# Stacked rounded latents and a one-pass key projection in an attention and expert kernel

## The reference, cut to what matters

```python
q = (x @ Wq + bq).reshape(B, T, H, D)
kv_latent = gelu(x @ Wkd + bkd)            # 64 columns
lat = kv_latent[..., :32] + kv_latent[..., 32:]
kv = lat @ Wku + bku                       # 32 rows, 256 columns
k, v = kv[..., :C], kv[..., C:]
attn = softmax(causal(q k^T * scale)); out = attn @ v
```

## Time and profile before

| | us |
|---|---|
| median of 3 runs | 648.69 |
| the runs | 646.8, 648.73, 648.69 |
| the profiled execution | 646.88 |
| its span in the trace | 645.0 |
| TensorE busy | 599.1 |
| VectorE busy | 542.1 |
| ScalarE busy | 487.6 |
| GpSimd busy | 167.7 |

### The profile page before, as it was taken

One profiled execution on the slowest core, in us unless ns is written; L12 is line 12 of the kernel. 1 busy time (PEld: TensorE's weight loads), 2 busy tenths in 40 slices (PEclk: granted clock), 3 DMA queues, 4 the chain that ended last, 5 costly groups with the idle time before them and its releaser, 6 DMA issues.

```text
span 645.0 us, 10999 instructions
## 1 busy us (share of the span) xinstructions
PE 599.1 (93%) x3297; PEld 441.4 (68%) x3297; DVE 542.1 (84%) x1338; ACT 487.6 (76%) x858; POOL 167.7 (26%) x144
## 2 busy tenths in 40 slices
PE   8799889888999999999999999785898999999996
PEld 5466556555545688888888888354675888888884
DVE  4868888888858868988988888869799789999997
ACT  5658999999647899999999999798635556666663
POOL 4422323223304033553455342040432000000000
PEclk9899999999998999999999999996897999999998
DMA  7000000000100042112201210000000222222201
GB/s 252 1 1 3 1 3 1 1 0 1 34 1 0 6 164 99 52 47 99 98 29 68 98 49 1 1 1 1 0 1 2 69 91 89 91 90 90 91 0 67
DMA packets 6491, 28.83 MB, mean 45 GB/s; under 512 B 862, under 2 KB 990, under 8 KB 4383
## 3 DMA queue, kind: packets, MB, share of 16 engines
q1 hardware_dynamic: 6448, 28.32, 12.4%
HBM read 27.13 MB, written 1.19 MB: 44 GB/s over the span
## 4 chain that ended last, share of the span: by engine, by line
PE 63%; DVE 24%; ACT 6%; issue 4%; DMA 1%; POOL 0%; SPq 0%; DVEq 0%; ACTq 0%; POOLq 0%
PE PS L1213 17%; PE PS L1215 16%; PE PS L1214 16%; DVE STAT L874 9%; PE PS L1364 2%; PE PS L1292 2%; DVE RA L894 2%; PE PS L1319 2%; PE PS L1239 2%; DVE SU L900 1%; DVE HN L680 1%; PE PS L1333 1%; ACT STAT L397 1%; DVE HL L692 1%; ACT RA L635 1%
## 5 line engine op out<-in xcount | busy, mean ns | idle before, releaser
L1015 DVE TENSOR_TENSOR RA<-AR,RA 128x512 fp32r<-128x512 f32 x144 | 137.4, 978 | 26.2 <-ACT RA L518 24.6
L517 ACT ACTIVATE AR<-PS,BI 128x512 f32<-128x512 f32 x144 | 99.8, 693 | 15.3 <-PE PS L1215 7.8
L1213 PE MATMUL PS<-HH,WH 128*128 128x512 f32 x272 | 108.9, 400 | 0.2
L1215 PE MATMUL PS<-HL,WH 128*128 128x512 f32 x272 | 107.1, 394 | 0.0
L1214 PE MATMUL PS<-HH,WL 128*128 128x512 f32 x272 | 107.1, 394 | 0.0
L518 ACT ACTIVATE RA<-PS,BI 128x512 fp32r<-128x512 f32 x144 | 98.7, 685 | 0.0
L874 DVE CUSTOM_DVE_ANT_0 STAT<-PS,MQ 128x128 f32<-128x128 f32 (+1 forms) x256 | 76.3, 355 | 20.0 <-PE PS L1320 19.9
L1213 PE MATMUL PS<-RA,WH 128*128 128x512 f32 x208 | 83.0, 399 | 3.7 <-DVE RA L1179 2.1
L1215 PE MATMUL PS<-RA,WH 128*128 128x512 f32 x208 | 81.2, 391 | 0.0
L1214 PE MATMUL PS<-RA,WL 128*128 128x512 f32 x208 | 81.2, 391 | 0.0
L320 POOL TENSOR_TENSOR AR<-AR 128x512 f32<-128x512 f32 x32 | 50.8, 1587 | 113.2 <-DVE AR L827 113.2
(11 more groups left out here) (212 smaller groups left out, 1164.3 us busy)
## 6 DMA issues: line engine op xcount, KB each, us to landing
AR<-comb SPq DMA_DIRECT2D x15, 1024.0 KB, 4.7
WS<-in_w SPq DMA_DIRECT2D x9, 512.0 KB, 5.5
WS<-in_w SPq DMA_DIRECT2D x7, 384.0 KB, 3.1
M<-in_mats SPq DMA_DIRECT2D x1, 1384.0 KB, 10.8
X<-in_xT SPq DMA_DIRECT2D x4, 256.0 KB, 4.4
out_xT<-X SPq DMA_DIRECT2D x4, 256.0 KB, 2.1
AR<-in_wmod SPq DMA_DIRECT2D x1, 768.0 KB, 7.8
AR<-in_w SPq DMA_DIRECT2D x1, 384.0 KB, 3.1
```

Of the source, the lines that this page charges most:

```text
L517: act.activation(G[:, c, :], PS[:, c, :], ACT.Gelu_apprx_tanh, bias=bias).then_inc(s["act"], 1)
L1015: dve.tensor_tensor(out=GL[:, m0 % 2, c, :], in0=G[:, c, :], in1=f(GH[:, m0 % 2, c, :]), op=ALU.subtract).then_inc(s["lo"], 1)
L1213: pe.matmul(out, wh, xh, start=first, stop=False)
L1215: return pe.matmul(out, wh, xl, start=False, stop=last)
```

## The change

The latents are no longer kept as the gelu's two halves in plain f32. The gelu goes to `LG`. A selection matmul (`three_rows`, `pick` in columns 640 to 737 of `KM`) writes the sum of the halves three times, and two rows of ones, to 98 rows of PSUM. One instruction (VectorE for block 0, ScalarE for blocks 1 to 3) rounds it into `LATR`, and one of VectorE makes `LAT` in fp32r: rounded, rest, rounded. The key and value weights get the matching rows (`KMS`: rounded, rounded, rest) by two VectorE instructions. One fp32r matmul of 98 rows then gives the split product. The latents of blocks 1 to 3 are made after the first projection. `LL` is made in four quarters in the steps 28 to 31 of the last expert instead of at the start.

```diff
-        KM = sb("KM", [65, 640])
+        LG = AR[0:65, 8192:10240]
+        KM = AR[0:98, 2048:2786]
+        LAT = RA[0:98, 3072:5120]
+        KMS = RA[0:98, 5120:5760]
+        KMR = RA[0:98, 5760:6400]
+        LATR = RA[0:98, 6400:7936].rearrange("p (r n) -> p r n", r=3)
+        SUM_BANK, VALUE_BANK = (0, 4, 2, 3), (5, 4, 2, 3)
 # GpSimd
+            gp.wait_ge(l_done, 1)
             gp.tensor_scalar(LH[:, :], lm, 1.0, 0.0, ALU.mult, ALU.add).then_inc(l1_split, 1)
-            gp.wait_ge(l1_split, 1)
-            gp.wait_ge(hn_done, 8)
-            gp.tensor_tensor(out=LL[:, :], in0=lm, in1=f(LH[:, :]), op=ALU.subtract).then_inc(l1_split, 1)
 # GpSimd, experts, after acc(m, ...)
+                    if m >= 28 and ne == 9:
+                        gp.wait_ge(l1_split, 1)
+                        part = slice((m - 28) * MATS["l1"] // 4, (m - 27) * MATS["l1"] // 4)
+                        gp.tensor_tensor(out=LL[:, part], in0=lm[:, part], in1=f(LH[:, part]), op=ALU.subtract)\
+                          .then_inc(l1_split, 1)
 # ScalarE
+            def rounded_latents(t):
+                act.wait_ge(sel_psum, t + 1)
+                if t == 3:
+                    act.wait_ge(l_done, 1)
+                act.activation(LATR[:, t % 3, :], PS[0:98, SUM_BANK[t], :], ACT.Copy, scale=vec("lat_sign")[0:98, :])\
+                   .then_inc(lr_more, 1)
             evac_proj(0, 0)
+            for t in range(1, NBLK):
+                rounded_latents(t)
             evac_proj(1, 1)
 # VectorE, before the modulation is copied
+            dve.tensor_scalar(KEPT[:, :], bias, vec("q_keep"), None, ALU.mult).then_inc(qk_bias, 1)
+            dve.tensor_scalar(SIGNED[:, :], bias, vec("q_sign"), -1.0, ALU.mult, ALU.mult).then_inc(qk_bias, 1)
+            dve.wait_ge(flipped, 2)
+            dve.tensor_scalar(KMR[:, 0:640], KM[:, 0:640], vec("w_sign")[0:98, :], None, ALU.mult).then_inc(kms_done, 1)
+            dve.wait_ge(kms_done, 1)
+            dve.scalar_tensor_tensor(out=KMS[:, 0:640], in0=KM[:, 0:640], scalar=vec("w_keep")[0:98, :], in1=f(KMR[:, 0:640]),
+                                     op0=ALU.mult, op1=ALU.subtract).then_inc(kms_done, 1)
 # VectorE, the latents
+            def latents(t):
+                if t == 0:
+                    dve.wait_ge(sel_psum, 1)
+                    dve.tensor_scalar(LATR[:, 0, :], PS[0:98, 0, :], vec("lat_sign")[0:98, :], None, ALU.mult)\
+                       .then_inc(lr_done, 1)
+                    dve.wait_ge(lr_done, 1)
+                else:
+                    dve.wait_ge(lr_more, t)
+                dve.scalar_tensor_tensor(out=blk(LAT, t), in0=PS[0:98, SUM_BANK[t], :], scalar=vec("lat_keep")[0:98, :],
+                                         in1=f(LATR[:, t % 3, :]), op0=ALU.mult, op1=ALU.subtract).then_inc(l_done, 1)
-            all_values(0)
-            all_values(1)
+            latents(1)
+            latents(2)
             maxima(0, 0, 0)
-            all_values(2)
+            latents(3)
             maxima(0, 0, 1)
             spread_max(0, 0)
+            all_values(0)
             with_max(0, 0)
-            all_values(3)
+            for j in range(1, 4):
+                all_values(j)
 # TensorE
+            def three_rows(t):
+                if t == 0:
+                    pe.wait_ge(in_k, 16)
+                    pe.wait_ge(latent_one, 1)
+                pe.wait_ge(lat_done, t + 1)
+                pe.matmul(PS[0:98, SUM_BANK[t], :], KM[0:65, 640:738], blk(LG, t), start=True, stop=True).then_inc(sel_psum, 1)
+            latent(0)
+            latent(1)
+            three_rows(0)
+            latent(2)
+            latent(3)
 # in project
-                pe.matmul(PS[:, 6, 256:512], KM[:, 128 * g:128 * g + 128], LAT[:, cols], start=True, stop=True)\
+                pe.matmul(PS[:, 6, 256:512], KMS[:, 128 * g:128 * g + 128], LAT[:, cols], start=True, stop=True)\
 # order before the first step
             project(0, 0, 0)
-            (16 value matmuls)
+            for t in range(1, NBLK):
+                three_rows(t)
             scores(0, 0, 0)
             project(1, 1, 0)
             scores(0, 0, 1)
             project(2, 2, 0)
-            keep_clock(8)
+            (16 value matmuls, fp32r, each four after l_done)
+            keep_clock(4)
             maxima_t(0, 0)
 # layer 1
-            pe.wait_ge(l1_split, 2)
+            pe.wait_ge(l1_split, 5)
```

More of the change, by code:

```diff
@@ L15 @@
 VECS = dict(bo=1, bq=4, q_sign=1, q_keep=1, k_keep=1, b1=4 * E0, b2=E0, pb=4, gb=3, fb=3,
-            outb=1, alpha=1, norm=1, norm2=1, bkd=1, c=16, prio=8)
+            outb=1, alpha=1, norm=1, norm2=1, bkd=1, c=16, prio=8,
+            w_sign=1, w_keep=1, lat_sign=1, lat_keep=1)
 MATS = dict(wkd=64, wq=512, wo=512, router=8, wg=8, l1=4 * 128 + 3 * 384)
@@ L92, in build @@
         ON = AR[:, 0:8192].rearrange("p (g n) -> p g n", g=4)
-        LAT = AR[0:65, 8192:10240]
+        LG = AR[0:65, 8192:10240]
+        KM = AR[0:98, 2048:2786]
         VALL = AR[:, 10240:12288].rearrange("p (i c) -> p i c", i=16)
@@ L155, in build @@
         latent_one = sem("latent_one")
+        kms_done, sel_psum, lr_done, lr_more, l_done = map(
+            sem, ("kms_done", "sel_psum", "lr_done", "lr_more", "l_done"))
         p1_psum, p1_done, a_done, asq_done, sa_done, hsi_done, sqrt_done, s_ready, scan_done, hs2_mul, hs2_done = map(
@@ L420, in _ @@
                 act.wait_ge(kd_done, t + 1)
-                act.activation(LAT[0:64, t * BLK:(t + 1) * BLK], PS[0:64, t, :], ACT.Gelu, bias=vec("bkd")[0:64, :])\
+                act.activation(LG[0:64, t * BLK:(t + 1) * BLK], PS[0:64, t, :], ACT.Gelu, bias=vec("bkd")[0:64, :])\
                    .then_inc(lat_done, 1)
@@ L829, in moe_scale @@
                    .then_inc(s["ymul"], 1)
-            dve.memset(LAT[64:65, :], 1.0).then_inc(latent_one, 1)
+            dve.memset(LG[64:65, :], 1.0).then_inc(latent_one, 1)
             dve.wait_ge(in_vec, 16)
@@ L834, in _ @@
                 centre(0, t)
+            bias = V[:, VAT["bq"]:VAT["bq"] + 4]
+            dve.tensor_scalar(KEPT[:, :], bias, vec("q_keep"), None, ALU.mult).then_inc(qk_bias, 1)
[5 more added lines that the diff above has]
+                                     op0=ALU.mult, op1=ALU.subtract).then_inc(kms_done, 1)
             dve.wait_ge(mod_psum, 1)
@@ L856, in _ @@
                 normalise(0, t)
+            def latents(t):
[8 more added lines that the diff above has]
+                                         in1=f(LATR[:, t % 3, :]), op0=ALU.mult, op1=ALU.subtract).then_inc(l_done, 1)
+            latents(0)
             def all_values(j):
@@ L1282, in _, with latent @@
             pe.wait_ge(in_mats, 16)
-            for t in range(NBLK):
+            def latent(t):
                 pe.wait_ge(hn_done, 2 * t + 2)
@@ L1391, in step @@
                     values(n - 1, n0 - 1, it)
-            pe.wait_ge(in_k, 16)
-            pe.wait_ge(lat_done, 1)
-            pe.wait_ge(latent_one, 1)
             pe.wait_ge(flipped, 4)
+            pe.wait_ge(kms_done, 2)
+            pe.wait_ge(l_done, 1)
             project(0, 0, 0)
[L1398 to L1403, removed]
+            for t in range(1, NBLK):
+                three_rows(t)
             pe.wait_ge(ident_done, 9)
@@ L1410, in _ @@
             project(2, 2, 0)
-            keep_clock(8)
+            for i in range(16):
+                if i % 4 == 0:
+                    pe.wait_ge(l_done, i // 4 + 1)
+                mm = pe.matmul(PS[:, VALUE_BANK[i // 4], 128 * (i % 4):128 * (i % 4) + 128],
+                               LAT[:, 128 * i:128 * i + 128], KMS[:, 512:640], start=True, stop=True)
+                if i % 4 == 3:
+                    mm.then_inc(v_psum, 1)
+            keep_clock(4)
             maxima_t(0, 0)
@@ L1681, in layouts @@
     put("bkd", a["L0_attn_bkd"])
+    put("w_sign", np.repeat(np.array([-1, -1, 1, -1, 1], f4), [32, 32, 32, 1, 1]))
+    put("w_keep", np.repeat(np.array([0, 0, 1, 0, 1], f4), [32, 32, 32, 1, 1]))
+    put("lat_sign", np.repeat(np.array([-1, 1, -1, -1], f4), [32, 32, 32, 2]))
+    put("lat_keep", np.repeat(np.array([0, 1, 0, 0], f4), [32, 32, 32, 2]))
     put("c", np.concatenate([a["L0_c"], a["L1_c"]]).T)
@@ L1694, in layouts @@
     wk = np.concatenate([heads(a["L0_attn_Wku"][:, :128], 3).reshape(32, 512), a["L0_attn_Wku"][:, 128:]], 1)
+    bias = np.concatenate([bk.reshape(1, 512), np.zeros((1, 128), f4)], 1)
+    pick = np.zeros((98, 98), f4)
+    pick[np.arange(192) % 64, np.arange(192) // 64 * 32 + np.arange(192) % 32] = 1.0
+    pick[64, 96:98] = 1.0
     rows = np.concatenate([a["L0_attn_bku"][128:], a["L0_ffn_router_b"]])
@@ L1704, in layouts @@
         mats=mats,
-        kmats=np.concatenate([wk, wk, np.concatenate([bk.reshape(1, 512), np.zeros((1, 128), f4)], 1)]),
+        kmats=np.concatenate([np.concatenate([wk, wk, wk, bias, bias]), pick], 1),
         rows=np.tile(rows, (128, 1)),
```

5 lines of the change are left out of this document (1 added, 4 removed).

## The result

The changed kernel takes 654.65 us (median of 4 runs, 654.22 to 658.81), beside 648.71 for the kernel before (646.8 to 649.72, 4 runs). The ratio is 1.0122, 95% interval 1.0098 to 1.0146: slower by 1.2%. Forecast were 650.3, a range from 646.0 to 652.8, and 0.39 for slower. The medians lie 5.9 us apart, where 1.6 were forecast. The direction of the forecast was right; the time lies outside the range.

What follows compares the result with a forecast made beforehand. Steady attention steps were taken as bound by VectorE, the start as serial, the experts' end as VectorE's. 646.88 + 1.1 - 0.3 + 1.6 = 649.3, plus half of the 1.9 between two run levels: 650.3 us, range 646.0 to 652.8.

Steps and rivals of the forecast that it cites:

- 1. One-pass key projection: Attention steps: 0.32 us less TensorE work per unit, worth nothing in steady steps, -0.3 over steps 0 to 2.
- 2. The start: Weights, latents and values before the first attention step: +1.1 us in sum, from +0.5 to +2.0.
- (b): When line 894 first runs: TensorE's clock falls near 30.5 and returns near 35, landing it between 36.1 and 36.9.
- -0.15: First run of line 894, against 36.65 before: forecast shift in us, from -0.55 to +0.25.
- 1.2 + 2.8 + 1.1: Before the first transposes: us for projection 2, sixteen value matmuls and four clock-keeping ones, mostly at 1.2 GHz, from 31.4.
- the order of `all_values`: Between line 894 and the first step: two more `all_values` of 0.65 each, +1.3 us.
- the two about the clock: Rivals at the start: clock stays up, 648.7 us, chance 0.22; clock late before the matmul at 20.7, 653, chance 0.08.
- The weights at 13.8: VectorE makes KMR and KMS before copying the modulation, moving that copy by about +0.6 us, 0 to +1.0.
- 3. `LL` in quarters: End of layer 0's experts: quarters 0 and 1 free, 2 costs +0.6, 3 costs +1.0; sum +1.6 us, +0.3 to +2.1.
- forecast +0.8: Up to the last attention unit: the start's +1.1 us and the key projection's -0.3 taken together.

Runs made afterwards that it cites:

- e11_before_dense: Kernel before, with two clock-keeping matmuls added ahead of scores(0,0,1) and three ahead of project(2): 646.79 us, ratio 0.9974.
- e6_v32: Changed kernel with its 16 value matmuls read as plain f32, two records each, instead of one-pass fp32r: 655.42 us, ratio 1.0126.
- e8_keep8: Changed kernel with eight clock-keeping matmuls behind the values instead of four: 656.76 us, ratio 1.0143.
- e2_values: Changed kernel with all four `all_values` ahead of `with_max` of unit 0, instead of one ahead and three behind: 654.27 us, ratio 1.0132.
- e7_all: Changed kernel with eight clock-keeping matmuls before the first scores, all `all_values` ahead of `with_max`, and `LL` quarters in steps 26 to 29: 649.65 us, ratio 1.0024.
- e13_dense_k32: e9_dense with the key projection read as plain f32 in all 32 units: 646.28 us, ratio 0.9981.
- e4_before_ll: Kernel before, with only `LL` made in four quarters in steps 28 to 31 instead of one instruction at 22 us: 648.73 us, ratio 1.0031.
- e1_fill: Changed kernel with eight clock-keeping matmuls where TensorE idles before the first scores: 652.68 us, ratio 1.0094.
- e5_fill_k32: e1_fill with the key projection read as plain f32 in every unit: 653.6 us, ratio 1.0075.
- e9_dense: e7_all with two more clock-keeping matmuls ahead of scores(0,0,1) and two ahead of project(2): 644.36 us, ratio 0.9952.

## Why the prediction was wrong, point by point

**1. One-pass key projection: mechanism right, size smaller.** Steady steps were worth nothing, as forecast: 125.34 against 125.36 for 27 units, and the two passes put back changed neither. The -0.3 for the steps 0 to 2 was too much: with the clock up, two passes and one give 18.05 and 18.07.

**2. The start. The step that failed is (b)**, "I expect the clock to fall at about 30.5 and to come back at about 35". It fell at 28.7 behind the idle time foreseen (the values' 3.73 us gone from 24.32), but it did not come back until 56. That the fall needs this gap is not shown: in e11_before_dense the clock fell at 28.6 with the values in place and 0.52 us idle. I had also read the fall in the kernel before as following three mostly idle microseconds; its trace shows TensorE busy for 1.00, 0.64 and 0.20 of the last three. My 35 was copied from the kernel before, without its matmuls: there TensorE came back to two f32 projection halves and eight long matmuls; here it came back to one f32 and one one-pass half, 16 short one-pass matmuls and four long ones. With the old values (e6_v32) or the old eight (e8_keep8) the clock returned by the first step; without the idle 1.58 us it did not (e2_values, e7_all). What decides on it stays open. I priced the lower clock for the matmuls ahead of line 894 alone, and took the steps behind it at 2.4 GHz. Line 894 came at 38.62, not at 36.1 to 36.9 (+1.97 on 36.65 in place of -0.15): my 1.2 + 2.8 + 1.1 from 31.4 ends ahead of the transposes, and measured were 1.24, 3.30, 1.82 and another 0.66 for the transposes, from 31.60. From there to unit 4 it took 24.96 instead of 18.75: +6.2. Of these 4.8 are the clock: e6_v32 and e8_keep8, which have the changed order and the clock back by the first step, take 20.20. The remaining 1.45 are the order of `all_values` (forecast +1.3). No rival held this: the two about the clock had it stay up, or come back late by one stretch at 20 us. What would have shown it: at half clock a step takes 6.66 (units 1 to 2, against 4.40), so that an uncertain return was worth 2.3 per step and not 1 us in all.

The weights at 13.8 cost 0.04 instead of 0.6 in this execution, since KMR and KMS took 0.55 and 0.88 and their data came no later than before. Elsewhere they did cost: in e13_dense_k32 TensorE had finished the modulation at 13.96, and the copy, behind KMS, started at 14.81.

**3. `LL` in quarters: right.** Forecast +1.6, measured +1.17 from step 30 to `centre`, in the changed kernel and alone (e4_before_ll); from unit 31 on it is +1.54 and +1.16, where the scatter ahead of step 30 comes in. A quarter takes 1.26 to 1.53, not 1.0, which my one row of 1664 columns undersized. Where it costs was right: 0.35 in step 30, 0.82 in the residual adds. Moved two steps ahead, the quarters cost 0.96 less up to `centre`; whether they cost anything there can't be told, since the kernels without them scatter by more.

**The sum.** 646.88 + 1.1 - 0.3 + 1.6 = 649.3 against 654.22 for the profiled execution. By terms: +8.16 up to the last unit (forecast +0.8), +1.54 to `centre` (forecast +1.6, and 1.17 of it the quarters'), and -2.3 in layer 1, where the recurrence's wait fell otherwise on the clock, which no term of mine held.

## What to carry to other kernels

Work taken off TensorE is not only worth its time: what it did for the clock goes with it. Here two ways of putting some of it back saved 4.8 us in the steps, at a cost of 2.4 ahead of them. Before such an edit, list TensorE's idle gaps in the new order, and price a fall of the clock for as long as the stage behind it lasts, not up to the next matmul. Filling one gap of several leaves it to chance (e1_fill, e5_fill_k32, e7_all); with all of them filled and `all_values` ahead, three profiled executions of three kept the clock from the first scores through the steps. Where a wait can't be shortened, fill it with matmuls that nobody reads (2.4 us in e1_fill, at no cost of their own: the scores start 1.78 us behind the selection matmuls, against 1.84 in the changed kernel), and put other engines' copies into time in which these wait anyway. A split on GpSimd that reads SBUF belongs in a stage in which VectorE has slack, not behind the last addition: two steps earlier it cost about 1 us less here.

## What the runs showed of the hardware that was not expected

- The clock stayed at 1.2 GHz for 27 us in which TensorE was busy most of the time (24.5 of the 27 us from 29 to 56, and without a break from 41 on). In e7_all it stayed there from 33 to 60.2 with no break at all. Work at hand was not enough to bring it back. In e6_v32 it came back 5 us after the f32 value matmuls had begun.
- Whether it falls differs between executions of one program: e7_all lies between 644.96 and 654.99, with mean clocks of 0.982 down to 0.956; e9_dense, with no gap over 0.3 us from its selection matmuls to the first step, within 2.5 us. The changed kernel and e2_values run the same program up to 33 us, but only e2_values had the clock low from 15.2 to 22.2.
- At 1.2 GHz 16 one-pass matmuls of 128 columns took 3.51 us, at 2.4 GHz 1.90, or 0.12 each (e9_dense); the 128-column f32 ones of two passes, 32 records, took 6.07 in e6_v32, most of it at the lower level.
